# Differential attention on one Trainium2 core: GpSimd forms the difference of all heads, and VectorE's list is reordered

## The chip, the core and the metric

The kernel runs on one core of a Trainium2 chip. The metric is the device time of one execution in microseconds (us), as the median of three runs. Lower is better. The core's engines run their own instruction lists side by side and meet only at semaphores: TensorE (PE, with its weight loads as PEld), VectorE (DVE), ScalarE (ACT), GpSimd (POOL) and the DMA queue that SyncE (SP) issues.

## What is computed

Eight layers follow each other on x of shape (8, 256, 256): four attention-like layers, each followed by a feed-forward layer, with a residual and a layer norm behind each. The change lies in the fourth attention, a differential attention with 16 heads of width 16, over the T = 256 tokens of each of B = 8 batch entries:

```
energy = jnp.einsum('bqhad,bkhad->bahqk', qd, kd)          # two maps a = 0, 1 for every head
energy = jnp.where(causal, NEG, energy)
scores = jax.nn.softmax(energy / np.sqrt(D), axis=-1)
lam = exp(sum(lq1*lk1)) - exp(sum(lq2*lk2)) + LAM_INIT      # one number a head
diff = scores[:, 0] - lam * scores[:, 1]
diff = jnp.where(causal, NEG, diff)
diff = jax.nn.softmax(diff, axis=-1)                        # a second softmax, over the difference
att = jnp.einsum('bhqv,bvhd->bqhd', diff, v)
att = att * rsqrt(mean(att*att) + EPS) * rms_w * (1 - LAM_INIT)
x = layernorm(x + att.reshape(b, s, E) @ Wo)
```

## The kernel before

The fourth attention is the function `l3_attention`. After the projections of q, k and v it goes through the 8 batch entries b, and for each through 8 **steps** i = 0 to 7. A step is one map a = i mod 2 of one quad r = i // 2 of four heads. The 256 query rows of a head lie on 128 partitions as two tiles t; the causal tile t = 0 has 128 keys and t = 1 has 256, so a head has 384 probabilities per partition. Each engine has a function `sequence(b)` that lists, step by step and by hand, what it does; the work for one quad is spread over later steps:

- **Step i, scores.** PE computes the scores of four heads into PSUM (`scores`, L1721) and adds the mask (L1725). The scores fill the four banks S, of which there is one copy: PE may start the scores of step i + 1 only when ACT has finished the exponentials of step i (semaphore `p_exp`). DVE takes the row maxima (`maxima`, L1961), ACT the exponentials and their sums (`exponentials`, L1864) into the buffer `pr[:, r, a]`.
- **After an even step** POOL masks the diagonal blocks of map 0 (`mask`, L1816, one instruction of 128x1024).
- **After an odd step** DVE makes the `ratios` (L1968 to L1970), by which map 1 is to be scaled for each row. Then the difference map 0 + ratio * map 1 is formed in two **units** of two heads each: unit A (heads 0 and 1) and unit B (heads 2 and 3). In each unit DVE takes the first head with two SCALAR_TENSOR_TENSOR instructions (`difference` in the vector block, L1979, 128x128 and 128x256), and POOL the second with three: two multiplications (L1826, 128x128 and 128x256) and, after a wait for them, an addition (L1829, 128x384). DVE does its head of unit A right behind the ratios, and its head of unit B behind the maxima of the next, even step.
- **Two steps later**, `second_maxima` on DVE takes the row maxima of a unit's difference (L1989, two reductions) and turns them into the bias of the second softmax (L1991, a tiny TENSOR_TENSOR of 128x4 with two inputs in SBUF, called the **bias instruction** below); ACT makes the second exponentials (`second`, L1881, four instructions).
- **Three steps later**, PE turns the unit (`turn`, L1736, six transposes), and ACT (L1872) and DVE (L1997) each copy one head out of PSUM.
- **Later still**: products with v (`values`, L1748 and L1751, odd steps), copied by DVE (L2002); turned back (`turn_back`, L1760, even steps) and divided by DVE (`take_output`, L2008 and L2009).
- **Once a batch entry**, for the entry before: POOL squares the output (`squares`, L1833, 128x512, in step 4); DVE does the RMS norm in step 5 (`norm_1`, `norm_2`: L2016, L2017, L81 to L88, L2022); PE turns the result in step 6 (`turn_output`, L1767), ACT copies it (`output`, L1887), PE projects it in step 7 (`project_output`, L1775), and DVE adds it to x and measures it (L108 to L121).

Three waits of that list matter below. In step 6 DVE's `take_output` waits for PE's `turn_output` (`oT_ps`); in step 7 PE's `values` waits for ACT's copy (`oT_ready`), since they use the same PSUM bank:

```python
if i == 6 and not opening:
    dve.wait_ge(oT_ps, b)
take_output(b, i)
...
if i == 7 and not opening:
    pe.wait_ge(oT_ready, b)
values(b, i)
```

and PE's `turn` of step i waits for the second exponentials that ACT made in step i - 1 (`p_ready`). The first batch entry (opening) has no norm and no output of an entry before; after the last one a closing sequence finishes the last quad.

## Time and profile before

| | |
|---|---|
| median of 3 runs | 3110.5 us (3109.22 to 3111.86) |
| profiled execution | 3111.67 us, of which 3109.9 us from the first to the last instruction |
| busy share of the span | PE 84%, DVE 60%, ACT 42%, POOL 12% |
| steps of the fourth attention | from about 2115 us to 2603 us of the span |
| granted TensorE clock, mean | 0.917 of full speed |

The profiled execution's own time is 1.2 us above the median and 1.8 us above its span. Shares over the whole span mix eight layers with different limits, so the fourth attention has to be read from its own stretch of the trace. Times in the trace count from the start of the span. An instruction's row gives start, duration, engine, line, operation and shapes; what stands in brackets is how long the engine sat idle before it and what ended the wait.

### The profile page before, as it was taken

To read this page: it belongs to the slowest core of one execution; us is meant where nothing else is said; L and a number is where in the kernel's file an instruction comes from. 1 tells how busy PE (TensorE), PEld (TensorE's weight loads), DVE (VectorE), ACT (ScalarE), POOL (GpSimd) and SP (SyncE) were. 2 spreads that over 40 slices of the span, in tenths; PEclk is the share of its full clock that TensorE was granted. 3 is DMA by queue.
4 is the path that set the end of the run, shared out by engine and by line. 5 is a ranking of instruction groups with operands and counts; after the bars stand their busy time and mean duration, and the time that the engine had idled before them with its cause. 6 is when DMAs were issued, how large, how long until landed. Compare 5 with 4: busy or idle time off the path is not lost. (4 is left out here: it accounts for less than half of the span.)

```text
span 3109.9 us, 43072 instructions
## 1 busy us (share of the span) xinstructions
PE 2608.6 (84%) x14256; PEld 1883.3 (61%) x14256; DVE 1858.5 (60%) x4295; ACT 1310.5 (42%) x3605; POOL 359.7 (12%) x392
## 2 busy tenths in 40 slices
PE   7988999889999999998698877796555654999997
PEld 5665544457776777677476665543443433877876
DVE  3665233445464555445645757546888886777777
ACT  4663455533443344334222132205777773332322
POOL 2440000000000000000121000003444440000000
PEclk9998999989999999999899888896777776999998
DMA  3002000000000000002000000100000003000000
GB/s 148 10 7 82 1 0 0 0 35 1 3 3 3 0 3 3 3 0 75 16 0 0 0 0 0 37 6 29 24 19 19 24 9 132 1 1 0 0 0 27
DMA packets 26415, 56.11 MB, mean 18 GB/s; under 512 B 3696, under 2 KB 22896, under 8 KB 24688
## 3 DMA queue, kind: packets, MB, share of 16 engines
q1 hardware_dynamic: 26352, 55.32, 4.8%
q8 instruction: 33, 0.54, 0.1%
q14 instruction: 30, 0.25, 0.0%
HBM read 39.59 MB, written 2.10 MB: 13 GB/s over the span
## 5 line engine op out<-in xcount | busy, mean ns | idle before, releaser
L1864 ACT ACTIVATE l3a_pr<-psum,l3a_nm 128x128 f32<-128x128 f32 (+1 forms) x512 | 207.1, 430 | 202.8 <-DVE l3a_nm L1961 202.8
L1721 PE MATMUL psum<-l3a_kr,l3a_qr 32*128 32x128 f32 (+1 forms) x1024 | 91.1, 491 | 180.3 <-ACT l3a_pr L1864 176.9
L108 DVE TENSOR_TENSOR x_sb<-psum,x_sb 128x512 f32 (+2 forms) x48 | 41.7, 868 | 235.2 <-PE psum L950 135.5
L757 DVE TENSOR_TENSOR l0f_hg<-l0f_sq,psum 128x512 f32<-128x512 f32 x128 | 87.8, 688 | 151.1 <-ACT l0f_sq L689 148.3
L1721 PEld LDWEIGHTS psum<-l3a_kr,l3a_qr 32*128 32x128 f32 x1024 | 51.5, 271 | 198.8 <-ACT l3a_pr L1864 186.3
L995 ACT ACTIVATE l1a_pr<-psum,l1a_nb,l1a_rq 128x128 f32<-128x128 f32 (+1 forms) x256 | 127.2, 509 | 87.2 <-DVE l1a_nb L1048 84.9
L1221 POOL TENSOR_TENSOR l1f_acc<-l1f_t 128x512 f32<-128x512 f32 x4 | 6.3, 1573 | 1334.3 <-DVE l1f_t L1284 1334.3
L2178 PE MATMUL psum<-l3f_x_hi,l3f_w_hi 128*128 x384 | 154.5, 402 | 6.6 <-DVE l3f_w_lo L2261 6.6
L2225 ACT ACTIVATE l3f_sg<-psum 128x512 f32<-128x512 f32 x96 | 57.3, 597 | 240.3 <-PE psum L2181 240.3
L1961 DVE TENSOR_REDUCE l3a_nm<-psum 128x2 f32<-128x256 f32 (+1 forms) x256 | 124.6, 548 | 53.9 <-PE psum L1725 53.9
L2179 PE MATMUL psum<-xT,l3f_w_hi 128*128 x384 | 152.9, 398 | 0.0
L2180 PE MATMUL psum<-l3f_x_hi,l3f_w_lo 128*128 x384 | 152.3, 397 | 0.0
L914 PE MATMUL psum<-l1a_kT,l1a_qT 128*128 128x128 f32 (+1 forms) x512 | 120.2, 359 | 20.9 <-ACT l1a_pr L995 14.0
L2192 PE MATMUL psum<-l3f_w_hi,l3f_h_hi 128*128 128x256 f32 x384 | 127.6, 332 | 7.9 <-DVE l3f_h_lo L2279 7.9
L1816 POOL TENSOR_TENSOR l3a_pr<-l3a_pr,w_l3a_mask 128x1024 f32<-128x1024 f32 x32 | 75.3, 2352 | 486.2 <-ACT l3a_pr L1864 486.2
L652 PE MATMUL psum<-l0f_hg,w_l0f_w 128*128 128x512 f32 x256 | 130.6, 593 | 0.8 <-DVE l0f_hg L757 0.8
L645 PE MATMUL psum<-l0f_xl,w_l0f_w 128*128 x256 | 130.6, 592 | 0.0
L1881 ACT ACTIVATE l3a_pr<-l3a_pr,l3a_nb,l3a_rec 128x128 f32<-128x128 f32 (+1 forms) x256 | 120.8, 581 | 3.8 <-DVE l3a_nb L1991 3.8
L885 PE MATMUL psum<-l1a_xc,w_l1a_q 128*128 128x256 f32 x512 | 122.4, 382 | 0.0
L687 ACT ACTIVATE l0f_relu<-psum 128x512 f32<-128x512 f32 x128 | 76.3, 596 | 108.8 <-PE psum L645 104.4
L867 PE MATMUL psum<-w_l1a_k,l1a_xc 128*128 128x512 f32 x256 | 112.8, 599 | 9.8 <-DMA l1a_xc<-xT 9.8
L891 PE MATMUL psum<-w_l1a_v,l1a_xc 128*128 128x512 f32 x256 | 120.3, 592 | 0.0
(424 smaller groups left out, 6942.2 us busy)
## 6 DMA issues: line engine op xcount, KB each, us to landing
w_l3f_all<-l3f_all_dram SPq DMA_DIRECT2D x1, 9216.0 KB, 25.7
l3a_qr<-l3a_q_all SPq DMA_DIRECT2D x32, 256.0 KB, 2.5
w_l0f_w<-l0f_w_dram SPq DMA_DIRECT2D x2, 2048.0 KB, 10.0
w_l1f_all<-l1f_all_dram SPq DMA_DIRECT2D x1, 2560.0 KB, 8.8
x_sb<-x_dram SPq DMA_DIRECT2D x1, 2048.0 KB, 8.5
l0a_xc<-xT SPq DMA_DIRECT2D x8, 256.0 KB, 2.5
w_l1a_q<-l1a_q_dram SPq DMA_DIRECT2D x1, 2048.0 KB, 7.9
w_l1a_k<-l1a_k_dram SPq DMA_DIRECT2D x1, 2048.0 KB, 13.5
```

Source lines behind the costliest of these rows:

```text
L645: mm(HB[e % 3], w["w1"][:, e, :], xl[:, chunk], start=True, stop=True).then_inc(h_ps, 1)
L652: mm(YL, w["w2"][:, e, :], hg[:, e % 2, :], start=(e == 0), stop=(e == E - 1)).then_inc(used, 1)
L885: last = mm(bank(2 + j % 2)[:, i * T:(i + 1) * T], w["q"][:, k, (2 * j + i) * HD:(2 * j + i + 1) * HD], xc[:, k, :], start=(k == 0), stop= ...
L995: last = nc.scalar.activation(pr[:, n % 2, i, s], S[n % 2][:, i, s], ACT.Exp, bias=nb[:, n % 2, t, i:i + 1], scale=rq[:, t, 2 * n + i:2 * ...
L1721: mm(S[:, g, t * P:t * P + (t + 1) * P], qr[rows, a, r, t * P:(t + 1) * P], kr[rows, a, 0:(t + 1) * P], start=(t == 0), stop=False, tile_p ...
L1864: last = nc.scalar.activation(pr[:, r, a, g, k], S[:, g, k], ACT.Exp, bias=nm[:, i % 2, g, t:t + 1], accum_out=sums[:, r, a, g, t:t + 1])
L1881: last = nc.scalar.activation(pr[:, r, 1, g, k], pr[:, r, 0, g, k], ACT.Exp, bias=nb2[:, r, g, t:t + 1], scale=rec[:, r, 0, g, t:t + 1])
L1961: last = nc.vector.tensor_reduce(nm[:, i % 2, 2 * pair:2 * pair + 2, t], S[:, 2 * pair:2 * pair + 2, t * P:t * P + (t + 1) * P], AX.X, ALU ...
L2178: mm(bk[e % 2], hi, x_hi[:, k, chunk], start=(k == 0), stop=False)
L2179: mm(bk[e % 2], hi, x_lo[:, k, chunk], start=False, stop=False)
L2180: mm(bk[e % 2], lo, x_hi[:, k, chunk], start=False, stop=(k == KD - 1))
L2192: mm(Y[:, t, :], h_hi[:, e % 2, tokens], hi, start=False, stop=False)
```

## The change

Both heads of a unit are now POOL's. Its three instructions per unit stay three, each over two heads at once (256, 512 and 768 elements per partition in place of 128, 256 and 384). DVE's `difference` is gone. In DVE's list `second_maxima` moves from right behind the maxima to behind the copies, the norm (step 5) and the output (step 7), just ahead of the ratios. One semaphore takes the place of two.

```diff
-        dif_even = sem("dif_even")
-        dif_odd = sem("dif_odd")
+        dif_ready = sem("dif_ready")
...
                 def difference(b, i):
                     s = b * NU + i
-                    r, g = i // 2, part(i).start + 1
+                    r, heads = i // 2, part(i)
                     if i % 2 == 0:
                         pool.wait_ge(ratio_ready, b * R + r + 1)
                         pool.wait_ge(masked, b * R + r + 1)
                     for t in range(TT):
                         k = slice(t * P, t * P + (t + 1) * P)
-                        last = nc.gpsimd.tensor_tensor(pr[:, r, 1, g, k], pr[:, r, 1, g, k], ratio[:, r, g, t:t + 1].broadcast_to((P, (t + 1) * P)), ALU.mult)
+                        last = nc.gpsimd.tensor_tensor(pr[:, r, 1, heads, k], pr[:, r, 1, heads, k], bc(ratio[:, r, heads, t], 2, (t + 1) * P), ALU.mult)
                     last.then_inc(scaled, 1)
                     pool.wait_ge(scaled, s + 1)
-                    nc.gpsimd.tensor_tensor(pr[:, r, 0, g, :], pr[:, r, 0, g, :], pr[:, r, 1, g, :], ALU.add).then_inc(dif_odd, 1)
+                    nc.gpsimd.tensor_tensor(pr[:, r, 0, heads, :], pr[:, r, 0, heads, :], pr[:, r, 1, heads, :], ALU.add).then_inc(dif_ready, 1)
...
-                def difference(b, i):
-                    r, g = i // 2 % R, part(i).start
-                    if i % 2 == 0:
-                        dve.wait_ge(ratio_ready, b * R + i // 2 + 1)
-                        dve.wait_ge(masked, b * R + i // 2 + 1)
-                    for t in range(TT):
-                        k = slice(t * P, t * P + (t + 1) * P)
-                        last = nc.vector.scalar_tensor_tensor(pr[:, r, 0, g, k], pr[:, r, 1, g, k], ratio[:, r, g, t:t + 1], pr[:, r, 0, g, k],
-                                                              ALU.mult, ALU.add)
-                    last.then_inc(dif_even, 1)
-
                 def second_maxima(b, i):
...
-                    dve.wait_ge(dif_even, s + 1)
-                    dve.wait_ge(dif_odd, s + 1)
+                    dve.wait_ge(dif_ready, s + 1)
...
-                        if live(i, 2, opening, closing):
-                            if i % 2 == 0:
-                                difference(b, i - 1)
-                            second_maxima(b, i)
...
+                        if live(i, 2, opening, closing):
+                            second_maxima(b, i)
                         if i % 2 == 1 and not closing:
                             ratios(b, i)
-                            difference(b, i - 1)
```

**VectorE, step 5** (maxima of step 5, then the norm). Before, its list begins so:

```order
L1961 TENSOR_REDUCE l3a_nm<-psum 128x2 x2
L1989 TENSOR_REDUCE l3a_nm<-l3a_pr 128x2 x2
L59 REGISTER_ALU
L1991 TENSOR_TENSOR l3a_nb<-l3a_nm,l3a_rec 128x4
L1996 ISA
L1997 COPY l3a_pt<-psum 128x384
L2002 COPY w_l3a_q<-psum 128x256
L2016 TENSOR_REDUCE l3a_vv<-w_l3a_q 128x32
```

In the changed kernel (`w_l3a_q` and `w_l3a_k` are the space of spent weights, here the output and v; L1960, L1976, L1978, L1984, L1989 and L2003 are the new numbers of L1961, L1989, L1991, L1997, L2002 and L2016):

```order
L1960 TENSOR_REDUCE l3a_nm<-psum 128x2 x2
L1983 ISA
L1984 COPY l3a_pt<-psum 128x384
L1988 REGISTER_ALU
L1989 COPY w_l3a_q<-psum 128x256
L2003 TENSOR_REDUCE l3a_vv<-w_l3a_q 128x32
```

The second maxima and the bias instruction are no longer between the maxima and the copies.

**VectorE, from the end of the norm in step 5 to the bias instruction of step 6.** Before:

```order
L2022 TENSOR_TENSOR w_l3a_q<-w_l3a_q,l3a_rs 128x512
L1967 REGISTER_ALU
L1968 RECIPROCAL l3a_rec<-l3a_sums 128x16
L59 REGISTER_ALU
L1969 TENSOR_TENSOR l3a_ratio<-l3a_sums,l3a_rec 128x8
L59 REGISTER_ALU
L1970 TENSOR_TENSOR l3a_ratio<-l3a_ratio,l3a_nlam 128x8
L1975 REGISTER_ALU
L1979 SCALAR_TENSOR_TENSOR l3a_pr<-l3a_pr,l3a_ratio 128x128
L1979 SCALAR_TENSOR_TENSOR l3a_pr<-l3a_pr,l3a_ratio 128x256
L1959 REGISTER_ALU
L1961 TENSOR_REDUCE l3a_nm<-psum 128x2 x2
```

In the changed kernel:

```order
L2009 TENSOR_TENSOR w_l3a_q<-w_l3a_q,l3a_rs 128x512
L1976 TENSOR_REDUCE l3a_nm<-l3a_pr 128x2 x2
L59 REGISTER_ALU
L1978 TENSOR_TENSOR l3a_nb<-l3a_nm,l3a_rec 128x4
L1966 REGISTER_ALU
L1967 RECIPROCAL l3a_rec<-l3a_sums 128x16
L59 REGISTER_ALU
L1968 TENSOR_TENSOR l3a_ratio<-l3a_sums,l3a_rec 128x8
L59 REGISTER_ALU
L1969 TENSOR_TENSOR l3a_ratio<-l3a_ratio,l3a_nlam 128x8
L1958 REGISTER_ALU
L1960 TENSOR_REDUCE l3a_nm<-psum 128x2 x2
```

The second maxima stand behind the norm and ahead of the ratios, and the two SCALAR_TENSOR_TENSOR between the ratios and the maxima of step 6 are gone.

**GpSimd, one unit**, before and in the changed kernel:

```order
L1826 TENSOR_TENSOR l3a_pr<-l3a_pr,l3a_ratio 128x128
L1826 TENSOR_TENSOR l3a_pr<-l3a_pr,l3a_ratio 128x256
L1828 REGISTER_ALU
L1829 TENSOR_TENSOR l3a_pr<-l3a_pr 128x384
```

```order
L1825 TENSOR_TENSOR l3a_pr<-l3a_pr,l3a_ratio 128x2x128
L1825 TENSOR_TENSOR l3a_pr<-l3a_pr,l3a_ratio 128x2x256
L1827 REGISTER_ALU
L1828 TENSOR_TENSOR l3a_pr<-l3a_pr 128x768
```

The order on GpSimd is as before; each instruction covers twice as much.

## Rows read from the trace of the kernel before

**Rows 1.** Busy us of PE, PEld, DVE, ACT, POOL, clock, DMA share, GB/s: one entry

```profile
2436.00:2494.00 58.00, 34.27 (x327) 23.08 (x325) 49.46 (x126) 44.00 (x169) 26.75 (x30) 0.76 0.06 20
```

**Rows 2.** Timeline of TensorE, steps 3 to 7 of that entry

```profile
2424.77 1.54 PE L1736 MATMUL psum<-cf_sb,l3a_pr 128*128 128x128 f32 x6
2427.44 0.94 PE L1721 MATMUL psum<-l3a_kr,l3a_qr 32*128 32x128 f32 x16 [1.13 <-ACT l3a_pr L1864]
...
2437.48 0.88 PE L1736 MATMUL psum<-cf_sb,l3a_pr 128*128 128x128 f32 x6
2440.48 1.66 PE L1721 MATMUL psum<-l3a_kr,l3a_qr 32*128 32x128 f32 x16 [2.12 <-ACT l3a_pr L1864]
...
2453.16 1.08 PE L1748 MATMUL psum<-l3a_pt,w_l3a_k 128*32 128x256 f32 x8 [0.16 <-issue]
```

**Rows 3.** Timeline of VectorE: copy of step 3, then steps 5 and 6

```profile
2426.42 0.56 DVE L1997 COPY l3a_pt<-psum 128x384 f32<-128x384 f32 x1 [0.34 <-PE psum L1736]
2436.04 1.95 DVE L1961 TENSOR_REDUCE l3a_nm<-psum 128x2 f32<-128x256 f32 x4 [2.00 <-PE psum L1725]
2437.91 1.00 DVE L1989 TENSOR_REDUCE l3a_nm<-l3a_pr 128x2 f32<-128x256 f32 x2
2439.42 0.54 DVE L1997 COPY l3a_pt<-psum 128x384 f32<-128x384 f32 x1
2440.21 0.67 DVE L2016 TENSOR_REDUCE l3a_vv<-w_l3a_q 128x32 f32<-128x512 f32 x1
2444.00 0.24 DVE L1968 RECIPROCAL l3a_rec<-l3a_sums 128x16 f32<-128x16 f32 x1
2444.68 1.34 DVE L1979 SCALAR_TENSOR_TENSOR l3a_pr<-l3a_pr,l3a_ratio 128x128 f32<-128x128 f32 x2
2445.95 1.94 DVE L1961 TENSOR_REDUCE l3a_nm<-psum 128x2 f32<-128x256 f32 x4
2449.20 1.00 DVE L1989 TENSOR_REDUCE l3a_nm<-l3a_pr 128x2 f32<-128x256 f32 x2
2450.34 0.56 DVE L1997 COPY l3a_pt<-psum 128x384 f32<-128x384 f32 x1
2451.05 0.29 DVE L2009 TENSOR_TENSOR w_l3a_q<-psum,l3a_recs 128x128 f32<-128x128 f32 x1
```

**Rows 4.** Timeline of ScalarE: steps 3, 4, 6 and 0, second exponentials of 6

```profile
2424.07 0.37 ACT L1864 ACTIVATE l3a_pr<-psum,l3a_nm 128x128 f32<-128x128 f32 x1 [1.24 <-DVE l3a_nm L1961]
2430.43 0.37 ACT L1864 ACTIVATE l3a_pr<-psum,l3a_nm 128x128 f32<-128x128 f32 x1 [0.92 <-DVE l3a_nm L1961]
2446.99 0.37 ACT L1864 ACTIVATE l3a_pr<-psum,l3a_nm 128x128 f32<-128x128 f32 x1 [4.45 <-DVE l3a_nm L1961]
2450.54 1.89 ACT L1881 ACTIVATE l3a_pr<-l3a_pr,l3a_nb,l3a_rec 128x128 f32<-128x128 f32 x4
2462.36 0.37 ACT L1864 ACTIVATE l3a_pr<-psum,l3a_nm 128x128 f32<-128x128 f32 x1 [3.25 <-DVE l3a_nm L1961]
```

**Rows 5.** Timeline of GpSimd, steps 4 and 5

```profile
2434.12 1.04 POOL L1833 TENSOR_TENSOR w_l3a_q<-w_l3a_q 128x512 f32<-128x512 f32 x1 [3.81 <-DVE w_l3a_q L2009]
2435.12 0.97 POOL L1826 TENSOR_TENSOR l3a_pr<-l3a_pr,l3a_ratio 128x128 f32<-128x128 f32 x2
2437.13 2.35 POOL L1816 TENSOR_TENSOR l3a_pr<-l3a_pr,w_l3a_mask 128x1024 f32<-128x1024 f32 x1
```

**Rows 6.** Timeline, steps 7 and 0: VectorE adds the output, then makes the ratios

```profile
2457.18 0.69 DVE L108 TENSOR_TENSOR x_sb<-psum,x_sb 128x512 f32 x1 [0.33 <-PE psum L1775]
...
2459.36 0.25 DVE L1968 RECIPROCAL l3a_rec<-l3a_sums 128x16 f32<-128x16 f32 x1
```

**Rows 7.** Timeline of the closing: GpSimd's addition, a bias instruction, the second exponentials

```profile
2579.05 0.99 POOL L1829 TENSOR_TENSOR l3a_pr<-l3a_pr 128x384 f32<-128x384 f32 x1
2579.46 0.60 DVE L1991 TENSOR_TENSOR l3a_nb<-l3a_nm,l3a_rec 128x4 f32<-128x4 f32 x1
2580.10 1.86 ACT L1881 ACTIVATE l3a_pr<-l3a_pr,l3a_nb,l3a_rec 128x128 f32<-128x128 f32 x4 [3.83 <-DVE l3a_nb L1991]
```

## The prediction

> **What bounds the kernel now.** The stretch table of the profile, taken over one batch entry of the fourth attention, shows 58.0 us in which VectorE is busy for 49.5, ScalarE for 44.0 and GpSimd for 26.8, at a granted TensorE clock of 0.76 [rows 1]. No engine is full, so the timelines decide, read one step at a time. In most steps a ring sets the pace: scores on TensorE, the maxima of the first two heads on VectorE, exponentials on ScalarE, the next scores. From one step's first exponentials to the next even step's is 6.36 us (2424.07 to 2430.43) [rows 4]. Two places are longer. I count t from the maxima of step 5 (2436.04). The maxima of step 6 start at t = 9.91, because VectorE works through its list without a pause: the norm from 4.17 to 7.96, the ratios, then the two SCALAR_TENSOR_TENSOR of 1.34 us [rows 3]. The exponentials of step 6 start at 10.95, those of the next entry's step 0 at 26.32 [rows 4]; before the latter VectorE waited for the projected output (add at 21.14, ratios from 23.32) [rows 6].
>
> **Step 5 to 6.** The copy (L1997) is now VectorE's first work behind the maxima. The transposes that it waits for end at 2438.36, so it starts at t = 2.4 [rows 2]. Copy and read-out take 0.79 us, the norm 3.79 [rows 3]: done at 7.0. Then the second maxima (1.14 us to the next instruction) and the ratios (0.68) [rows 3]: maxima of step 6 at 8.8, 1.1 earlier. This is what the removed 1.34 us buy less the wait for the transposes. But the bias instruction, done before the copy at 3.4 until now [rows 3], ends at 8.2, and ScalarE's second exponentials wait for it. They start 0.04 us behind and take 1.86 [rows 7], to 10.05; only then can the first exponentials of step 6 begin. Gain there: 0.9 us of the 1.1.
>
> **Step 6 to 7: two queues meet.** TensorE turns the unit of step 6 only when those second exponentials are done, from about 10.15. It has then idled for about 3 us, and behind 2.12 us of idling its scores already take 1.66 us against 0.94 behind 1.13 us [rows 2], so I take the slow level: six transposes 1.54 us as at 2424.77 [rows 2], the four of the output about 1.1, both done at 12.55. VectorE's division waits for them and takes 0.5 (copy and division together 1.00) [rows 3], the second maxima 1.04. The bias instruction thus asks at about 14.15.
>
> GpSimd's durations are not in this trace for the doubled shapes. Multiplications of 128 and 256 elements take 0.97 together and one of 512 takes 1.04, which is 0.15 us each plus 1.73 ns an element: 1.64 for 256 and 512. Additions: 384 in 0.99 [rows 7], 1024 in 2.35, so 768 in 1.8 [rows 5]. A unit is 3.5 us. The bounds are 2.0, if only the number of instructions counted, and 4.0, if all doubled; I take 3.5, since both fits have most of their cost per element. The units start at 8.85: A is ready at 12.35, B's multiplications end at 14.0, B's addition runs from 14.05 to 15.85.
>
> That matters because GpSimd and VectorE get in each other's way: the bias instruction of the closing, which started at 2579.46 inside an addition of GpSimd, took 0.60 us and ended with it at 2580.06 [rows 7], though it handles 4 elements. So my 14.15 against 14.05 is a tie. If it comes in just ahead of the addition, second exponentials start at 14.3 against 14.50 before [rows 4]. ScalarE's copy and TensorE's values product then come at 16.75 instead of 17.12 [rows 2]; from there to the add is 4.02 us as before, and 2.18 from the add to the end of the measuring [rows 2, 6]: 22.95. Here the moved second maxima cost what the removed instructions save, since they no longer lie under the wait for the projection: bias done at 24.15, second exponentials to 26.0, first exponentials of step 0 at 26.0 against 26.32. **0.3 us an entry, in 7 entries: 2.2 us.** So most of the 0.9 us is given back.
>
> **Even steps 2 and 4.** In the odd step before, the copy waits for TensorE until 2.35 us behind the first exponentials (2426.42) [rows 3, 4]; with 0.79 the second maxima start at 3.15 (before: ahead of the copy), the bias is ready at 4.35, second exponentials end at 6.2. VectorE's removed head would allow 6.0, so the next exponentials come at 6.2 instead of 6.36: 0.16, twice an entry, in the six entries (the third on) in which the even steps' scores run at the fast level, as at 2427.44 [rows 2]: **2 us**. GpSimd's longer unit is covered here: A is ready 3.5 us behind the ratios, when VectorE has finished maxima, copy and division, and its bias instruction asks 4.6 us behind them, inside B's multiplication (4.1 to 5.2).
>
> **Closing.** No other work covers the unit. The bias instruction of unit A ended at 2580.06 with GpSimd's addition [rows 7], two short units of 2.1 to 2.2 us, so some 4.4 to 4.5 us, behind the ratios; now it waits for 3.5 plus 1.04 and then for the end of B's multiplication, at about 5.2: **0.7 us lost**. Unit B, at 8.2, is just hidden by A's way over TensorE.
>
> **Sum.** The profiled execution is 3111.67 us, 1.2 above the median; the differences are worked out on its rows and taken off the median: 3110.5 - 2.2 - 2.0 + 0.7 = **3107.0 us**.
>
> GPSIMD Engine Reference, section 3, of the Trainium skill says that an elementwise tensor_tensor takes GpSimd 1.96 times as long as VectorE, and advises VectorE for such work. By its 4497 ns for 2048 elements a unit is an estimated 3.4 us, near the fit from rows. The rows show the same direction, 0.99 us for an addition of 384 [rows 7]. It speaks against the change as far as GpSimd's latency is not covered, which is the closing here and, in the rival below, step 6.
>
> **The rivals.**
>
> *The bias instruction of step 6 hits B's addition (slower).* It then ends with the addition at 15.87, and the second exponentials start 1.4 us later than before, at 15.9. ScalarE's copy holds up TensorE's values product until 18.35, 1.2 us later than before; TensorE has idled for over 2 us by then and may run values, transposes and part of the projection at the slow level, up to 0.8 more. Per entry 1.2 to 2.0, in 7 entries 8.4 to 14, less 2.0 and plus 0.7: 3117.6 to 3123.2. It decides at a difference of 0.1 us between two sums of some ten terms. For it: the numbers as they stand put the request 0.1 behind the addition's start. Against it: a slightly slower GpSimd, or faster transposes (0.88 us as at 2437.48 [rows 2]), puts it ahead.
>
> SBUF — State Buffer, section "Who interferes with whom", of the Trainium skill gives the rule behind this: a VectorE instruction with two SBUF inputs and a GpSimd one that reads SBUF exclude each other for the whole instruction. By that rule the whole addition of 1.8 us counts, not the moment of the meeting; the trace agrees, since the 0.60 us ended with GpSimd's 0.99 [rows 7].
>
> *The clock tips upward (faster).* TensorE's turn in the even steps comes about 0.8 us later, so it idles about 2.4 us instead of 3.4 before an odd step's scores. If these then run in 0.94 instead of 1.66 us, ScalarE's list becomes the limit, about 0.35 us a step and three steps an entry: 8 us more, 3099. Against it: 2.12 us of idling were enough for the slow level at 2440.48 [rows 2].
>
> *The gain arrives in full (faster).* If the wait for the projected output and the bias were hidden, 1.1 us in step 6 and 1.3 in step 0 would give 17 us: 3094. The add at 21.14 and its waiting are in the row, so I hold it for unlikely.
>
> *GpSimd is slower than 4 us a unit (slower).* Unit A is then late in every even step; at 5 us the second exponentials end about 1 us late in the even steps, three an entry: 3125 and more.
>
> **Chances.** Forecast 0.38; addition hit 0.30; slow GpSimd or other new waits 0.06; upward clock 0.14; full gain 0.12. A measurement of this kernel tells about 0.2%, 6.2 us, from no change. The forecast lies inside it; both faster rivals are outside, and so is the hit (7 to 13 us slower). Faster 0.26, same 0.38, slower 0.36. The range 3096 to 3123 takes in the clock and the hit. The forecast's own is 3102 to 3112.
>
> **What would show it.** L1979 gone; units of 3.5 us on GpSimd; exponentials of step 6 near t = 10.0 instead of 10.95; the bias instruction of step 6 with 0.1 to 0.3 us if I am right, over 1 us if it hits the addition; the exponentials of the next step 0 near 26.0. An entry should take 57.4 us; 59 or more would be the hit. What would make me wrong most easily is the 0.1 us above, and a TensorE clock that settles otherwise.

## The result: 0.9% slower

| | before | after |
|---|---|---|
| median of the runs (from, to), us | 3111.18 (3109.22 to 3112.91) | 3139.16 (3137.47 to 3140.69) |
| span of the profiled execution, us | 3109.9 | 3138.0 |
| granted clock, whole span | 0.917 | 0.905 |

The ratio is 1.009, with a 95% interval from 1.0072 to 1.0107. The forecast was 3107.0 us and its range went up to 3123; the measured time lies 16 us above that.

The stretch table over one entry of the fourth attention in the kernel after (columns as in [rows 1]; steps 5 of the fifth entry to 5 of the sixth):

```profile
2386.00:2446.00 60.00, 36.95 (x322) 24.84 (x322) 41.93 (x110) 43.95 (x169) 36.61 (x30) 0.67 0.06 20
```

The load moved as the change says: VectorE is busy for 41.9 us instead of 49.5, GpSimd for 36.6 instead of 26.8 [rows 1]. The entry is nevertheless longer, 60.54 us from the maxima of step 5 at 2385.64 to the next ones at 2446.18, where 58.0 us had passed before, and the granted clock fell from 0.76 to 0.67. In the rows below t counts from the maxima of step 5 at 2385.64.

VectorE's timeline of the kernel after, steps 5, 6, 7 and 0 in this stretch:

```profile
2388.98 0.56 DVE L1984 COPY l3a_pt<-psum 128x384 f32<-128x384 f32 x1 [1.39 <-PE psum L1735]
...
2393.57 1.00 DVE L1976 TENSOR_REDUCE l3a_nm<-l3a_pr 128x2 f32<-128x256 f32 x2
...
2395.30 1.95 DVE L1960 TENSOR_REDUCE l3a_nm<-psum 128x2 f32<-128x256 f32 x4
...
2399.61 1.00 DVE L1976 TENSOR_REDUCE l3a_nm<-l3a_pr 128x2 f32<-128x256 f32 x2
2400.64 1.78 DVE L1978 TENSOR_TENSOR l3a_nb<-l3a_nm,l3a_rec 128x4 f32<-128x4 f32 x1
...
2410.99 0.69 DVE L108 TENSOR_TENSOR x_sb<-psum,x_sb 128x512 f32 x1 [2.04 <-PE psum L1774]
...
2413.14 1.01 DVE L1976 TENSOR_REDUCE l3a_nm<-l3a_pr 128x2 f32<-128x256 f32 x2
```

GpSimd's timeline there, the difference of unit B of the quad:

```profile
2398.91 1.62 POOL L1825 TENSOR_TENSOR l3a_pr<-l3a_pr,l3a_ratio 128x256 f32<-128x256 f32 x2
2400.60 1.80 POOL L1828 TENSOR_TENSOR l3a_pr<-l3a_pr 128x768 f32<-128x768 f32 x1
```

ScalarE's: first exponentials of step 6, second exponentials of step 6, first exponentials of step 0:

```profile
2396.58 0.35 ACT L1863 ACTIVATE l3a_pr<-psum,l3a_nm 128x128 f32<-128x128 f32 x1
...
2402.46 1.86 ACT L1880 ACTIVATE l3a_pr<-l3a_pr,l3a_nb,l3a_rec 128x128 f32<-128x128 f32 x4 [2.20 <-DVE l3a_nb L1978]
...
2416.33 0.37 ACT L1863 ACTIVATE l3a_pr<-psum,l3a_nm 128x128 f32<-128x128 f32 x1
```

TensorE's: transposes of step 5, then the values product and the output's projection of step 7:

```profile
2387.40 1.54 PE L1735 MATMUL psum<-cf_sb,l3a_pr 128*128 128x128 f32 x6
...
2405.04 1.08 PE L1747 MATMUL psum<-l3a_pt,w_l3a_k 128*32 128x256 f32 x8 [2.49 <-ACT w_l3a_q L1886]
...
2407.81 3.01 PE L1774 MATMUL psum<-l3a_wo,w_l3a_q 128*128 128x256 f32 x8
```

Read them as a chain. The bias instruction (L1978, four elements a partition) starts at 2400.64, 0.04 us after GpSimd's addition, and lasts 1.78 us, to the end of the addition at 2402.40. The second exponentials start at once behind it, at t = 16.82, where the kernel before had 14.50 [rows 4]. The values product follows at 19.40 instead of 17.12 [rows 2], after 2.49 us of idling. The transposes and most of the projection behind it run at the slow level: the projection takes 3.01 us, where the same eight matmuls took 1.89 us before; the scores of step 0 behind it are fast again (0.94 us at 2410.75). The output's addition is at t = 25.35 instead of 21.14 [rows 6], the exponentials of step 0 at 30.69 instead of 26.32 [rows 4].

Where the 28.1 us of span went, from the rows' own times: the maxima of step 7 of the last entry stand at 2584.04 instead of 2568.59, which is 15.4 us (0.3 of them from ahead of the attention); from there to the first instruction of the next layer it takes 43.1 instead of 34.65 us, 8.5; and the rest of the program 510.8 instead of 506.7, 4.2.

### The profile page after: what moved, and what is told of

Its sections match the earlier page's. It is cut to its first block and busy times, and to the rows that moved or that the text cites. A ratio compares the mean times of both kernels' runs of the same rounds, so it can differ in the third digit from the quotient of the medians.

```text
span 3138.0 us, 42836 instructions
## 1 busy us (share of the span) xinstructions
PE 2633.9 (84%) x14256; PEld 1902.9 (61%) x14256; DVE 1800.2 (57%) x4167; ACT 1313.9 (42%) x3605; POOL 445.9 (14%) x392
## 5 line engine op out<-in xcount | busy, mean ns | idle before, releaser
L1960 DVE TENSOR_REDUCE l3a_nm<-psum 128x2 f32<-128x256 f32 (+1 forms) x256 | 124.8, 550 | 67.7 <-PE psum L1724 65.9
L1735 PE MATMUL psum<-cf_sb,l3a_pr 128*128 128x128 f32 x384 | 84.9, 382 | 63.2 <-ACT l3a_pr L1880 62.9
L1825 POOL TENSOR_TENSOR l3a_pr<-l3a_pr,l3a_ratio 128x256 f32<-128x256 f32 (+1 forms) x128 | 103.2, 828 | 174.8 <-DVE l3a_ratio L1969 174.8
L374 POOL TENSOR_TENSOR l0a_pr<-l0a_pr,l0a_rec 128x256 f32<-128x256 f32 (+1 forms) x128 | 101.9, 828 | 141.8 <-DVE l0a_rec L464 141.8
```

The lines of the kernel that those rows point to most:

```text
L1960: last = nc.vector.tensor_reduce(nm[:, i % 2, 2 * pair:2 * pair + 2, t], S[:, 2 * pair:2 * pair + 2, t * P:t * P + (t + 1) * P], AX.X, ALU ...
```

## The experiments

The times are medians; "entry" and "closing" are read from the profiled execution, which lies up to 4.8 us from the median (run 7: 3112.2 us, its fastest). "Entry" is the time between the maxima of step 5 of two entries, mean of the last five, "closing" that from the last maxima of step 7 to the first instruction of the next layer's norm.

| version | us | ratio to before (95%) | entry | closing |
|---|---|---|---|---|
| before | 3111.2 | 1 | 58.1 | 34.7 |
| after | 3139.2 | 1.009 (1.0072 to 1.0107) | 60.8 | 43.1 |
| 1 GpSimd alone | 3110.9 | 0.9996 (0.9986 to 1.0006) | 58.0 | 37.9 |
| 2 order alone | 3165.9 | 1.0173 (1.0156 to 1.019) | 65.0 | 42.3 |
| 3 late in even steps only | 3108.1 | 0.9987 (0.9978 to 0.9997) | 57.6 | 37.8 |
| 4 addition in two | 3119.1 | 1.003 (1.0021 to 1.004) | 58.0 | 41.9 |
| 5 step 6 first | 3122.1 | 1.0032 (1.0019 to 1.0044) | 59.1 | 42.2 |
| 6 closing early | 3134.0 | 1.0072 (1.0058 to 1.0085) | 60.8 | 40.2 |
| 7 step 5 early | 3117.0 | 1.0022 (1.0013 to 1.0031) | 57.9 | 42.1 |
| 8 ratios first, steps 5 and 7 | 3130.2 | 1.0066 (1.0052 to 1.008) | 61.1 | 34.2 |
| 9 ratios first, step 7 | 3097.4 | 0.9957 (0.9944 to 0.9971) | 57.1 | 34.9 |
| 10 as 9, addition in two | 3098.5 | 0.9963 (0.9949 to 0.9976) | 57.2 | 35.0 |
| 11 before, ratios first in 7 | 3112.1 | 1.0003 (0.9994 to 1.0012) | 58.4 | 35.0 |

### 1 and 2: the two halves of the change apart

Run 1 takes the kernel after and puts the second maxima back to their old place:

```diff
+                        if live(i, 2, opening, closing):
+                            second_maxima(b, i)
                         if live(i, 3, opening, closing):
...
-                        if live(i, 2, opening, closing):
-                            second_maxima(b, i)
                         if i % 2 == 1 and not closing:
                             ratios(b, i)
```

> GpSimd forms all differences, but VectorE's second maxima stay at their old place, right behind the maxima, in every step (the two SCALAR_TENSOR_TENSOR are gone). Theory 'order' (the loss comes from moving the second maxima behind copies that wait for TensorE, so that second exponentials, transposes, copy and second maxima follow each other in one chain): most of the 28 us goes away, the closing is near the old length, 3105 to 3116 us; what stays is that in step 4 the second maxima wait 3.5 us for unit A ahead of the division, which puts GpSimd's squares and unit B later. Theory 'GpSimd' (the doubled unit itself is too slow): 3130 us or more.

Run 2 takes the kernel before, keeps VectorE's head of each unit there, and moves the second maxima alone:

```diff
-                        if live(i, 2, opening, closing):
-                            if i % 2 == 0:
-                                difference(b, i - 1)
-                            second_maxima(b, i)
+                        if live(i, 2, opening, closing) and i % 2 == 0:
+                            difference(b, i - 1)
...
+                        if live(i, 2, opening, closing):
+                            second_maxima(b, i)
                         if i % 2 == 1 and not closing:
                             ratios(b, i)
```

> VectorE keeps its head of every unit, and only the second maxima move to behind copies, norm and output. Theory 'order': slower than before although GpSimd's instructions are the short ones, 3122 to 3138 us, with the second exponentials of step 6 late, the closing some 5 to 8 us longer. Theory 'hit' (the loss is the bias instruction that waits for a 1.8 us addition of GpSimd): no instruction of GpSimd is that long here but the mask, so 3108 to 3118 us.

Measured: 3110.9 us, as the theory "order" had it, and 3165.9 us, outside both ranges. Giving GpSimd the whole difference costs nothing and gains nothing when the list keeps its order. The order alone costs 55 us, more than any rival had for the whole change. The two do not add up (28 together): with the late order, giving GpSimd the whole difference wins back 27 us, half of what the order loses. Part of the 55 us are meetings again, with GpSimd's mask and not with an addition: in steps 0, 2 and 6 of every entry behind the first the bias instruction takes 1.62 to 1.79 us, 21 times. At 0.16 us for one alone these are an estimated 31 of the 55 us. VectorE's and GpSimd's timelines of one of them, step 6:

```profile
2418.49 1.63 DVE L1991 TENSOR_TENSOR l3a_nb<-l3a_nm,l3a_rec 128x4 f32<-128x4 f32 x1
...
2425.76 0.56 DVE L1997 COPY l3a_pt<-psum 128x384 f32<-128x384 f32 x1 [3.44 <-PE psum L1736]
```

```profile
2417.75 2.35 POOL L1816 TENSOR_TENSOR l3a_pr<-l3a_pr,w_l3a_mask 128x1024 f32<-128x1024 f32 x1 [1.40 <-ACT l3a_pr L1864]
```

It ends at 2420.12 with the mask (2420.10). The copy of step 7 then waits 3.44 us for TensorE, and the maxima of step 0 come 30.3 to 30.9 us behind those of step 5, against 25.2 to 25.5 before (third entry on).

### 3: late in even steps only

```diff
+                        if live(i, 2, opening, closing) and (i % 2 == 1 or closing):
+                            second_maxima(b, i)
                         if live(i, 3, opening, closing):
...
-                        if live(i, 2, opening, closing):
+                        if live(i, 2, opening, closing) and not (i % 2 == 1 or closing):
                             second_maxima(b, i)
```

> GpSimd forms all differences. The second maxima stand right behind the maxima in odd steps and in the closing, where unit B is ready by then, and behind copy and division in even steps, where unit A is ready only 3.5 us behind the ratios. Both theories: norm and output no longer stand ahead of a bias. Step 6's maxima about 1.2 us earlier than in the kernel before, step 0's too: 3092 to 3102 us if the bias instruction of step 6 comes in ahead of the addition, which it should, since the second exponentials of step 5 are on time and the transposes no longer late. Theory 'GpSimd': 3115 us or more.

Measured: 3108.1 us, between the two ranges that were expected. Step 5 to 6 gained even more than my 1.1 us (8.35 us between the maxima, 9.91 before), but step 7 to 0 gave it back (10.7 us, 8.7 before). TensorE's timeline in steps 7 and 0:

```profile
2447.31 1.08 PE L1747 MATMUL psum<-l3a_pt,w_l3a_k 128*32 128x256 f32 x8 [0.78 <-ACT w_l3a_q L1886]
...
2450.09 3.43 PE L1774 MATMUL psum<-l3a_wo,w_l3a_q 128*128 128x256 f32 x8
```

The same eight matmuls take 1.89 us in the kernel before. GpSimd had then stood still for 7.73 us waiting for the ratios, which VectorE makes behind the output. That suggested runs 8 and 9.

### 4 and 5: the meeting in step 6

Run 4 leaves the list as it is after the change and makes GpSimd's addition of 1.80 us two of 384 elements:

```diff
-                    nc.gpsimd.tensor_tensor(pr[:, r, 0, heads, :], pr[:, r, 0, heads, :], pr[:, r, 1, heads, :], ALU.add).then_inc(dif_ready, 1)
+                    for h in range(heads.start, heads.stop):
+                        last = nc.gpsimd.tensor_tensor(pr[:, r, 0, h, :], pr[:, r, 0, h, :], pr[:, r, 1, h, :], ALU.add)
+                    last.then_inc(dif_ready, 1)
```

> The kernel after the change, but GpSimd's addition of a unit (128x768, 1.80 us) is made as two instructions of 128x384 (the kernel before had one of about 1.0 to 1.1 us a head). Theory A, that what the bias instruction of step 6 pays is the rest of the GpSimd instruction that it meets: the bias instruction falls from 1.75 to 1.78 us to at most 1.1, and each of the seven entries loses 0.7 to 1.2 us less: 3130 to 3135 us. Theory B, that the late second maxima cost through their place alone and the met instruction is only a symptom: 3137 to 3142 us, a little more where the two additions together are longer than one.

Run 5 puts the second maxima of step 6 ahead of the division:

```diff
+                        if i == 6 and not opening and not closing:
+                            second_maxima(b, i)
                         if i % 2 == 0 and live(i, 6, opening, closing):
                             if i == 6 and not opening:
                                 dve.wait_ge(oT_ps, b)
                             take_output(b, i)
...
-                        if live(i, 2, opening, closing):
+                        if live(i, 2, opening, closing) and not (i == 6 and not opening and not closing):
                             second_maxima(b, i)
```

> The changed kernel, but in step 6 the second maxima stand ahead of the division (which waits for TensorE's turn_output) instead of behind it. The bias instruction then asks about 0.6 us earlier, inside the multiplication of 512, and should end 1.8 us earlier (at most 0.6 us long instead of 1.77). Theory 'hit': second exponentials of step 6 are 1.9 us earlier in 7 entries and TensorE idles 1.9 us less before the values product; 13 us back at least, up to 25 with the clock: 3113 to 3126 us. Theory 'order' alone: 3132 us or more.

Measured: 3119.1 and 3122.1 us. VectorE's timeline of run 4, steps 5 and 6:

```profile
2436.44 0.56 DVE L1986 COPY l3a_pt<-psum 128x384 f32<-128x384 f32 x1 [0.46 <-PE psum L1735]
...
2442.75 1.95 DVE L1962 TENSOR_REDUCE l3a_nm<-psum 128x2 f32<-128x256 f32 x4
...
2446.57 1.01 DVE L1978 TENSOR_REDUCE l3a_nm<-l3a_pr 128x2 f32<-128x256 f32 x2 [0.48 <-POOL l3a_pr L1829]
2447.62 0.50 DVE L1980 TENSOR_TENSOR l3a_nb<-l3a_nm,l3a_rec 128x4 f32<-128x4 f32 x1
```

Run 5 came out as its theory "hit" said. Run 4 gains 20 us, outside the ranges of both its theories, and it does not show what it was made for: the bias instruction never meets one of the halved additions. In the row above it meets B's multiplications (2446.49 to 2448.11) and ends with them. In the second and seventh entries it asks 5.34 us behind the maxima of step 6, as after the change, but unit A now takes 0.15 us longer on GpSimd, and the request comes in just ahead of the addition. VectorE's and GpSimd's timelines of run 4, second entry:

```profile
2214.64 0.16 DVE L1980 TENSOR_TENSOR l3a_nb<-l3a_nm,l3a_rec 128x4 f32<-128x4 f32 x1
```

```profile
2213.05 1.60 POOL L1825 TENSOR_TENSOR l3a_pr<-l3a_pr,l3a_ratio 128x256 f32<-128x256 f32 x2
2214.73 1.95 POOL L1829 TENSOR_TENSOR l3a_pr<-l3a_pr 128x384 f32<-128x384 f32 x2
```

So it is the 0.15 us by which GpSimd got slower that breaks the tie in these two. In the other five entries it asks 4.8 to 4.9 us behind the maxima of step 6, behind transposes at the fast level; why they are fast there is not isolated, and whether a shorter addition helps, this run leaves open. In its whole trace no bias instruction takes over 1.0 us; in that of the kernel after eleven take 1.64 to 1.78 us, seven in step 6 and four in step 2. At about 1.3 us each these are an estimated 14 us of the 20.

In the entry whose rows are shown, the maxima of step 5 are at 2434.03. The copy stands at 2.41 behind them, where I had put it, and the maxima of step 6 at 8.72: TensorE's transposes ran in 0.87 us and not in 1.54. Of the 2.7 us by which its second exponentials of step 6 come earlier (t = 14.13 against 16.82), 0.9 come with the maxima of step 6, 1.3 from the bias instruction, and 0.5 from the transposes of step 6. Run 5 takes the meeting away and mostly keeps the late step 5 (maxima of step 6 at 8.8 to 9.7). VectorE's timeline of an entry with 9.66:

```profile
2453.36 0.51 DVE L1978 TENSOR_TENSOR l3a_nb<-l3a_nm,l3a_rec 128x4 f32<-128x4 f32 x1
```

Its entries are 59.1 us in the mean, 1.8 under the 60.8 after the change: so much is the meeting of step 6 worth, within what the rival allowed (1.2 to 2.0). Both have 9.38 us in the mean from the maxima of step 5 to those of step 6, and both have a meeting in step 2 in four entries. Of the 1.0 us that is left to the 58.0 of run 4, 0.7 stand between the same maxima (8.69 us in run 4); that the rest goes with the late step 5 too is not shown.

### 6 and 7: closing and step 5

The edit is that of run 3, with `closing` or `i == 5` as the condition for the early place:

```diff
+                        if live(i, 2, opening, closing) and (closing):
```

> The kernel after the change, with the second maxima at their old place (ahead of the copies) in the closing steps alone. Theory A, that the closing steps are a chain of their own in which each unit's second maxima now wait for the transposes of the unit before: the stretch from the last maxima (7,7) to the first instruction of the next layer's norm falls from 43.1 us back to 34.5 to 36, and the time is 3129 to 3133 us. Theory B, that the closing steps are long because the entries end late with the engines out of step: the stretch stays above 41 us and the time at 3137 us or more.

```diff
+                        if live(i, 2, opening, closing) and (i == 5):
```

> The kernel after the change, with the second maxima at their old place in step 5 alone, so that they stand ahead of the copies and of the norm. Theory A, that part of an entry's loss comes from step 5, where the second maxima end the norm's stretch and hold ratios and the maxima of step 6: maxima of step 6 come 0.8 to 1.3 us earlier (9.66 us after those of step 5 now, 8.3 to 8.9 then), and 3124 to 3132 us. Theory B, that steps 6 and 0 alone decide (second maxima behind the output and its wait for TensorE): step 7 and step 0 give back what step 6 gains, 3136 to 3141 us.

Run 6: 3134.0 us, 5 less than after, and just outside the 3129 to 3133 us of theory A; the closing is 40.2 us, not the 34.5 to 36 of that theory, so the order explains 2.9 of its 8.5 us in this kernel and not nearly all. The rest shows in VectorE's timeline of run 6, the first unit of the closing:

```profile
2596.65 1.01 DVE L1976 TENSOR_REDUCE l3a_nm<-l3a_pr 128x2 f32<-128x256 f32 x2 [3.61 <-POOL l3a_pr L1828]
```

VectorE waits 3.61 us for GpSimd, whose difference cannot start before the ratios, and these stand behind the output. Run 7: 3117.0 us, 22 less, more than either theory allowed. VectorE's maxima of step 6 and TensorE's projection:

```profile
2439.00 1.95 DVE L1960 TENSOR_REDUCE l3a_nm<-psum 128x2 f32<-128x256 f32 x4
```

```profile
2449.63 2.76 PE L1774 MATMUL psum<-l3a_wo,w_l3a_q 128*128 128x256 f32 x8
```

The maxima of step 6 stand 8.64 us behind those of step 5 although the transposes of step 5 are slow here too (1.54 us at 2432.12): with the second maxima ahead of the copy their wait is filled with work. VectorE then comes to the second maxima of step 6 before GpSimd has unit A (it waits 0.82 us), and the bias instruction has 0.50 us: it asks 4.73 us behind the maxima of step 6, in B's multiplication, not 5.34 as after the change. With this one move the meeting of step 6 is gone, too.

### 8 to 11: an earlier start for GpSimd

Run 8 is run 3 with the ratios of step 5 between the halves of the norm and those of step 7 ahead of the output (its old call stays for steps 1 and 3):

```diff
                                 norm_1(b - 1)
+                                if not closing:
+                                    ratios(b, i)
                                 norm_2(b - 1)
...
                             if i == 7:
+                                if not closing:
+                                    ratios(b, i)
                                 output(b - 1)
...
-                        if i % 2 == 1 and not closing:
+                        if i % 2 == 1 and not closing and (opening or i < 4):
                             ratios(b, i)
```

> The version with the second maxima early in odd steps and in the closing and late in even steps (3108.1 us), and VectorE's ratios of step 5 between the two halves of the norm, and those of step 7 ahead of the output instead of behind it. Theory A, that GpSimd's late start in step 6 and step 0 (it waits 5.2 and 7.7 us for the ratios) is what holds the second maxima of step 6 (they wait 0.81 us for GpSimd) and lets TensorE fall to its slow clock for the output projection (3.43 us): GpSimd begins 2.5 to 5 us earlier, period of step 0 falls from 10.7 us to 8.7 to 10, and 3094 to 3103 us. Theory B, that GpSimd's start is covered by other work, or that its locks only fall on other VectorE instructions: 3105 to 3111 us.

Measured: 3130.2 us, 22 more than run 3 and outside both ranges. It is the clearest view of the two engines' quarrel. VectorE's timeline, part of the norm in step 5:

```profile
2448.69 0.61 DVE L84 TENSOR_TENSOR l3a_tmp<-l3a_rs 128x32 f32<-128x32 f32 x1
2449.34 0.96 DVE L86 SCALAR_TENSOR_TENSOR l3a_tmp<-l3a_vv,l3a_tmp 128x32 f32<-128x32 f32 x1
2450.34 0.19 DVE L88 SCALAR_TENSOR_TENSOR l3a_rs<-l3a_tmp,l3a_rs 128x32 f32<-128x32 f32 x1
2450.57 1.68 DVE L84 TENSOR_TENSOR l3a_tmp<-l3a_rs 128x32 f32<-128x32 f32 x1
```

GpSimd's timeline at the same time:

```profile
2448.65 1.61 POOL L1825 TENSOR_TENSOR l3a_pr<-l3a_pr,l3a_ratio 128x256 f32<-128x256 f32 x2 [2.49 <-DVE l3a_ratio L1969]
2450.34 1.86 POOL L1828 TENSOR_TENSOR l3a_pr<-l3a_pr 128x768 f32<-128x768 f32 x1
```

Each tiny instruction of the norm that starts inside a GpSimd instruction (0.19 us alone) ends with it: 2449.30 and 2450.30 with the two multiplications, 2452.25 with the addition (2452.20). The one at 2450.34, which starts together with the addition, takes its 0.19 us. From the first of the ten (2448.49) to the end of the last it is 7.5 us, against 2.2 in run 3, and the maxima of step 6 come at 13.8 to 14.7. In step 7, with hardly anything tiny to meet, the other half worked: 8.6 us from the maxima of step 7 to those of step 0, against 10.7 in run 3.

Run 9 keeps that half alone; run 10 adds the split addition of run 4; run 11 makes the edit of step 7 (the first four lines below) in the kernel before.

```diff
                             if i == 7:
+                                if not closing:
+                                    ratios(b, i)
                                 output(b - 1)
...
-                        if i % 2 == 1 and not closing:
+                        if i % 2 == 1 and not closing and (opening or i < 7):
                             ratios(b, i)
```

> The version of 3108.1 us (second maxima early in odd steps and in the closing, late in even steps), with VectorE's ratios of step 7 ahead of the output; those of step 5 stay behind the norm. Theory A, that GpSimd's early start in step 5 cost the 22 us of the run before this one, since each of the norm's tiny VectorE instructions met a GpSimd instruction, and that the one in step 7 was a gain: period of step 6 8.3 to 8.5 us, of step 0 8.5 to 9.0 (10.7 without the edit), 3090 to 3098 us. Theory B, that step 0 was short there only because step 6 was long: period of step 0 9.8 or more, 3102 to 3109 us.

```diff
+                    for h in range(heads.start, heads.stop):
+                        last = nc.gpsimd.tensor_tensor(pr[:, r, 0, h, :], pr[:, r, 0, h, :], pr[:, r, 1, h, :], ALU.add)
+                    last.then_inc(dif_ready, 1)
```

> The same, and GpSimd's addition of a unit as two instructions of 128x384, which shortens what a VectorE instruction waits when it meets one (0.51 instead of 1.78 us in the split version of the kernel after the change) and makes GpSimd's unit 0.15 us longer. With the second maxima early in odd steps the bias instruction meets an addition less often, so 0 to 4 us under the unsplit one if the meeting counts here too, and 1 to 3 us above it if only the longer unit counts.

```diff
                         if i % 2 == 1 and not closing:
-                            ratios(b, i)
+                            if opening or i < 7:
+                                ratios(b, i)
                             difference(b, i - 1)
```

> The kernel before the change, with VectorE's ratios of step 7 ahead of the output instead of behind it and nothing else: a control of whether this edit needs GpSimd's longer difference to pay. Period of step 0 is 8.7 us before. Theory A, that in the kernel before the maxima of step 0 wait for VectorE's copies and the output, not for GpSimd: 3108 to 3112 us, no change. Theory B, that GpSimd's start (and VectorE's shorter list ahead of the maxima of step 0) was on the path there too: 3100 to 3107 us.

Measured: 3097.4, 3098.5 and 3112.1 us. Run 9 beats both kernels: 14 us under the one before, 11 under run 3. VectorE's timeline of it in step 7 of the sixth entry, and GpSimd's:

```profile
2446.55 0.24 DVE L1967 RECIPROCAL l3a_rec<-l3a_sums 128x16 f32<-128x16 f32 x1
...
2448.25 0.69 DVE L108 TENSOR_TENSOR x_sb<-psum,x_sb 128x512 f32 x1 [1.06 <-PE psum L1774]
...
2450.85 1.95 DVE L1960 TENSOR_REDUCE l3a_nm<-psum 128x2 f32<-128x256 f32 x4
```

```profile
2447.27 1.61 POOL L1825 TENSOR_TENSOR l3a_pr<-l3a_pr,l3a_ratio 128x256 f32<-128x256 f32 x2 [2.99 <-DVE l3a_ratio L1969]
```

The ratios fill VectorE's wait for the projection, GpSimd starts about a microsecond before the output is added, and the next entry's maxima follow at 2450.85, 9.3 us behind those of step 7. That is among the best of its entries: the mean is 9.7 us (9.15 to 10.2), 10.6 in run 3. The expected 8.5 to 9.0 was not reached, and the projection is still slow (2.58 us here, 3.3 to 3.5 in entries of 9.7 to 10.2). The closing gains 2.9 us. Of the 14 us under the kernel before, about 2 lie in the rest of the program, where nothing was edited. Run 11 shows that the edit is worth nothing in the kernel before, as its theory A said: it pays in the list of run 3, where GpSimd has the longer work. Splitting the addition on top (run 10) changes nothing that can be told.

## Why the prediction was wrong

**What held.** GpSimd's durations: 1.61 to 1.62 us for the two multiplications and 1.80 to 1.82 for the addition, where I had 1.64 and 1.8. That a meeting lasts to the end of GpSimd's instruction: 1.78 us at 2400.64, for an instruction that has 0.16 alone. SBUF — State Buffer, section "Who interferes with whom", of the Trainium skill adds that reductions never take part; the traces agree, a pair of second maxima took 1.00 to 1.02 us in every run, whatever GpSimd did. The transposes of step 6 and the output's at the slow level, 1.54 and 1.06 us. And the place where it would be decided: the bias instruction of step 6 against B's addition.

**The tie (step 6 to 7).** My numbers had the addition 0.1 us ahead of the request, and I chose the other side. It is ahead by 0.04 to 0.08 us, in each of the seven entries. The bias instruction has 1.75 to 1.78 us every time. What looked like a chance of 30% is a locked pattern: GpSimd starts behind the ratios, and VectorE's request ends a chain that starts at the bias instruction of step 5, just ahead of the ratios, so that a delay of the one delays the other. In the sixth entry the maxima of step 6 come 0.80 us earlier than in the fifth, and the bias instruction takes 1.77 us all the same. VectorE's timeline:

```profile
2446.18 1.95 DVE L1960 TENSOR_REDUCE l3a_nm<-psum 128x2 f32<-128x256 f32 x4 [1.53 <-PE psum L1724]
2448.72 0.56 DVE L1984 COPY l3a_pt<-psum 128x384 f32<-128x384 f32 x1 [0.59 <-PE psum L1735]
...
2455.04 1.95 DVE L1960 TENSOR_REDUCE l3a_nm<-psum 128x2 f32<-128x256 f32 x4
...
2460.39 1.77 DVE L1978 TENSOR_TENSOR l3a_nb<-l3a_nm,l3a_rec 128x4 f32<-128x4 f32 x1
```

The forecast's side of the tie had a slip besides: it put the values product 2.45 us behind the start of the second exponentials (14.3 to 16.75), where the rows have 2.62 (14.50 to 17.12) [rows 2, 4] and the kernel after has 2.58. Its 0.3 us an entry would have been some 0.15.

**The copy in step 5.** I took t = 2.4 from transposes of 0.88 us; they took 1.54 and the copy stands at 3.34. That makes the maxima of step 6 9.66 instead of 8.8, and it alone undid the gain: the exponentials of step 6 came at 10.94 (2396.58), as before, not at 10.05. So it is in five of the seven entries; in the sixth, with transposes of 0.87 us, the copy stands at 2.54 and the exponentials of step 6 come at 10.14, as forecast. I had allowed for the slow level in step 6 and not in step 5.

**Values to addition (step 7).** Taken as 4.02 us as before, up to 0.8 more in the rival. It is 5.95 (19.40 to 25.35), 1.9 more, of which 1.1 are the projection's 3.01 against 1.89 us and 0.7 the transposes' 1.54 against 0.88. With the 2.3 us by which the second exponentials are late, this is the whole of the 4.37 us by which step 0 is late; 0.2 come behind the addition. The rival's price for an entry, 1.2 to 2.0, is what the meeting is worth (1.8, run 5), but it left out the late step 5 beside it: the second exponentials are 2.3 us late, not 1.4.

**Even steps 2 and 4.** Forecast 0.3 us an entry. From the exponentials of step 1 to those of step 5 it takes 25.13 instead of 26.08, so 0.95 in the fifth entry (others 24.2 to 26.3): the clock tipped upward in one odd step, the mechanism of my first faster rival, in one step of its three. TensorE's timeline, scores of step 3:

```profile
2370.98 0.94 PE L1720 MATMUL psum<-l3a_kr,l3a_qr 32*128 32x128 f32 x16 [2.30 <-ACT l3a_pr L1863]
```

They ran at the fast level behind 2.30 us of idling, though I had held against that rival that 2.12 us were enough for the slow one. I also took the bias instruction of the even steps to be safe in B's multiplication; in step 2 of four entries it met the addition (1.64 to 1.78 us).

**Closing.** Forecast +0.7, measured +8.5. ScalarE's timeline of the kernel after, second exponentials of three units that follow each other, and below it a row of the kernel before:

```profile
2595.28 1.86 ACT L1880 ACTIVATE l3a_pr<-l3a_pr,l3a_nb,l3a_rec 128x128 f32<-128x128 f32 x4 [5.20 <-DVE l3a_nb L1978]
2601.00 1.86 ACT L1880 ACTIVATE l3a_pr<-l3a_pr,l3a_nb,l3a_rec 128x128 f32<-128x128 f32 x4 [2.32 <-DVE l3a_nb L1978]
2606.60 1.86 ACT L1880 ACTIVATE l3a_pr<-l3a_pr,l3a_nb,l3a_rec 128x128 f32<-128x128 f32 x4 [2.20 <-DVE l3a_nb L1978]
```

```profile
2583.50 1.85 ACT L1881 ACTIVATE l3a_pr<-l3a_pr,l3a_nb,l3a_rec 128x128 f32<-128x128 f32 x4
```

After the change they come every 5.6 to 5.7 us; before, the first two were 3.4 apart (2580.10 [rows 7] and 2583.50). I priced only GpSimd's longer unit and not the moved second maxima, which now stand behind the copy of the unit before, so that two units can't overlap. Of the 8.5 us, 2.9 are this order in the closing (run 6), another 2.4 go with the order in the odd steps (40.2 us in run 6, 37.8 in run 3, which has them early too), and 2.9 with the late start of GpSimd behind the output (37.8 us in run 3, 34.9 in run 9, the same list but for the ratios).

**The rest of the program.** I expected nothing; it took 4.2 us more. In the other versions it lies between 504 and 511 us, in no order that follows the edits (505.9 in run 2, 510.4 in run 4), so this part is neither explained nor tied to the change.

**Not settled.** Why the transposes of step 5 run at the slow level in the kernel after and at the fast one in run 4. Two entries of the kernel after have them at 0.87 and 0.94 us, too, so it is not the list alone; no run isolates what decides. The meeting does not hang on it.

## What to carry to other kernels

A tiny instruction that two engines' queues hang on must not stand where the other engine runs its longest one; price such a meeting at the whole remaining length, and if both sides start from the same event, treat it as certain or excluded rather than as a chance. When an instruction is moved behind a wait, cost the places where nothing else overlaps (closing, opening) apart, and each wait twice, at either level of TensorE's clock. If work goes to a slower engine, look first for what releases it: here three instructions that start it, moved into a wait, won 11 us (run 3 to run 9), where the old order in odd steps and in the closing had only made good the 28 us lost and 3 more.

## Seen on the way

- Runs 4, 5 and 7 each win back 17 to 22 of 28 us with quite different edits. In all three the bias instruction of step 6 takes 0.16 to 0.51 us: they undo the same meeting, so their gains can't be added up.
- Making each GpSimd unit 0.15 us slower, with two additions for one, took 20 us off the kernel after (run 4): in two entries that alone let the bias instruction in ahead of the addition.
- The same eight matmuls of the output's projection took 1.89 us before, 3.01 after and 3.43 in run 3, behind 0.16, 2.49 and 0.78 us of idling ahead of the values product: the idling just before does not tell the level alone.
- In run 8 six VectorE instructions of 32 elements a partition that need 0.19 us each cost 5.3 us more between them by meeting GpSimd.
